# A two-layer Chebyshev graph network: one gathered chunk per step, an unrolled walk, a second table of h W2_1, dense stages that lag a visit each

## The chip, the cores and the metric

One NeuronCore of a Trainium2 chip. The metric is device time in microseconds, the median of plain runs, without the profiler.

## The reference

```
norm  = -dinv[src] * dinv[dst]                # dinv = 1/sqrt(number of edges leaving a node)
prop(h) = segment_sum(h[src] * norm, dst)     # 106250 edges sorted by dst, 6250 nodes
h1 = x @ W1_0 + prop(x) @ W1_1 + b1           # x: 6250 x 512 fp32, the weights 512 x 512
h  = leaky(layer_norm(h1) * gamma + beta)     # slope 0.01
y  = h @ W2_0 + prop(h) @ W2_1 + b2
out = layernorm(x + y)                        # without gamma and beta
```

Each node has 17 edges on average, so propagation is what costs: for every edge a row of 512 values is fetched by index and added into its node's row.

## The kernel before, in words

Nodes lie in 49 tiles of 128 (`TILES`), edges in 832 chunks of 128 (`CHUNKS`). The result must be near fp32, so a table in HBM holds every row as two fp16 halves, high and low, scaled by dinv and a power of two: `table[l]`, one per layer, 2 KB a row, 256 KB a chunk. One chunk is fetched by one indirect DMA on GpSimd (`L444`) into `ring`, 8 slots of a group of two chunks each.

**Steps.** Edges are sorted by destination, so a tile's edges are a run of groups. The walk has 464 steps per layer (`STEPS`): 416 groups (`GROUPS`) and 48 tile borders; a group on a border is stepped over once for each of its two tiles, but gathered once. Which tile and group a step has depends on the data: counts made in the start stage stand in `tile_i`, `group_i` and `slot_i` and are loaded into registers, 8 steps at a time. One step is: VectorE makes two one-hot matrices (edge x node in the tile, `L923`), PE multiplies them with the two chunks' high and low halves into one of 4 PSUM banks (`L710`, 4 matmuls), VectorE adds the bank, times `down` (dinv and the sign), to the tile's sums in `acc` (`L947`). `acc` holds all 49 tiles on chip.

PE may not write a bank before its add of four steps ago is done (`sums_added`). The sequence of a slot is relayed by SyncE: it waits for a group's landing, raises `groups_ready` for PE, waits for the step after which the slot is unused (`steps_done`, `L392`) and raises `ring_free` for GpSimd (`L393`). SyncE also copies the indices of 16 chunks at a time into `index` (`L371`).

**Blocks and visits.** The walk is run in blocks of 8 steps on PE and VectorE (`walk`, `L278`). After nearly every block each engine makes one *visit*, the dense stage of one tile whose sums must be complete by then; if an input's borders lay too late, `early` would send its visit behind the walk. The order of work in each engine's queue is that order of the code. On VectorE the one-hots of the next block stand right behind the visit (`prepare`). A visit in layer 0 is, for tile v:

```
...
                        for c in range(KB):
                            nc.tensor.matmul(to[:, :], base_in[:, tile_slot, c * P:(c + 1) * P],
                                             wB[:, c * D:(c + 1) * D], start=c == 0, stop=False)
                        pe.wait_ge(staged_ready, TILES * l + it.n + 1)
                        wait(pe, turned_moved, TILES * l + it.n)
                        turn(staged[tile_slot], bank[TURN_BANK], sums_turned)
...
                        pe.wait_ge(turned_moved, TILES * l + it.n + 1)
...
```

that is: PE multiplies the tile's features, read back already turned from `feat_dram`, with wB (`L727`); ScalarE copies the sums out of `acc` (`L546`); PE turns them with 4 transposes (`L655`, called from `L731`); ScalarE moves them to SBUF (`L564`); PE waits for that and multiplies with wA (`L749`); ScalarE copies the result to `acc` (`L613`). Other lines of the same visit work on older tiles: statistics (`L991`, `L994`), reciprocal and shift (`L958`, `L960`), normalising (`L556`), turning (`L736`), gamma and beta (`L598`), leaky (`L967`), turning back (`L742`), the split into high and low half (`L608`, `L974`), and the stores of features and of the second table. Layer 1's visit has the same two products and ends with the residual (`L983`), statistics and the output store. fp32 products take two PE instructions per 128 rows, so four blocks of weights are eight instructions. ScalarE issues the loads and stores of the visits.

Ahead of the walk a start stage of some 200 us loads x, counts degrees and borders, turns x into `feat_dram[0]` and writes the first table.

Of the kernel before, what the change touches and what calls it, by code (L numbers as in the profile page):

```python
# [17 lines left out]
WALK_FITS = "a step's tile is a count of at most TILES - 1 bounds, and its group the rest of its number"  # L39
# [36 lines left out]
def gnn_resnorm_kernel(nc, x, src, dst, w1_0, w1_1, b1, gamma, beta, w2_0, w2_1, b2, out):  # L76
# [7 lines left out]
    GROUP = 2  # L84
    GROUPS = -(-E // (GROUP * P))
    CHUNKS = GROUPS * GROUP
    STEPS = GROUPS + BOUNDS
    UNROLL = 8
    STEP_BLOCKS = STEPS // UNROLL
    GATHER_BLOCKS = GROUPS // UNROLL  # L90
    RING = UNROLL
    FREE_LAG = 4
# [3 lines left out]
    TABLE_VISIT = HIST_VISITS + 2  # L96
    LOAD = 7
    LOADS = TILES // LOAD
    FIRST_PLACE = 2
    PER = 6  # L100
    PERIODS = TILES // PER
    BIAS_PARTS = 3

    LAG_STATS, LAG_NORMAL, LAG_HIDDEN, LAG_LEAKY, LAG_BACK, LAG_LOW = 1, 2, 3, 4, 5, 6
# [4 lines left out]
    WALK = STEPS + 2 * UNROLL  # L109
    assert STEPS % UNROLL == 0 and GROUPS % (2 * UNROLL) == 0 and HIST * HIST_VISITS <= COLS  # L110
    assert HIST * HIST_VISITS * P >= E and TILES == LOADS * LOAD == 49 and CHUNKS <= COLS and TILES == PER * PERIODS + 1
    assert STEP_BLOCKS == FIRST_PLACE + (PER + 1) * PERIODS
# [6 lines left out]
    with ctx:  # L119
# [7 lines left out]
        ring = sb("ring", [P, RING * GROUP * ROW], FP16)  # L127
        wA = sb("wA", [P, KB * D], FP32)
        wB = sb("wB", [P, KB * D], FP32)
        work = sb("work", [P, 8 * D], FP32)  # L130
# [7 lines left out]
        count_i = sb("count_i", [P, WALK], I32)  # L138
        count = sb("count", [P, WALK], FP32)
        count_h = sb("count_h", [P, P], FP16)  # L140
        part_i = sb("part_i", [P, 1], I32)
        part = sb("part", [P, 1], FP32)
        thr = sb("thr", [P, TILES], FP32)
        onehot = sb("onehot", [P, UNROLL, GROUP, P], FP16)
        dst_c = sb("dst_c", [P, COLS], FP32)
        src_u = sb("src_u", [P, COLS], U32)
        src_lo = base_in[:, 0, 0:COLS // 2].bitcast(BF16)
        src_hi = base_in[:, 1, 0:COLS // 2].bitcast(BF16)
        index = sb("index", [P, 2, UNROLL * GROUP], U32)
        below = sb("below", [P, TILES], FP32)  # L150
        neg_tile = sb("neg_tile", [P, WALK], FP32)
        tile_i = sb("tile_i", [1, WALK], I32)
        group_i = sb("group_i", [1, WALK], I32)
        slot_i = sb("slot_i", [1, WALK], I32)
        used_i = sb("used_i", [1, GROUPS], I32)
# [864 lines left out]
```

## Time and profile before

| | |
|---|---|
| plain runs (3) | median 2442.14 us, 2441.22 to 2442.58 |
| profiled execution, span from first to last instruction | 3370.7 us |
| PE busy | 2065.1 us, 7250 matmuls |
| VectorE busy | 1544.4 us, 3507 instructions |
| ScalarE busy | 505.3 us |
| GpSimd busy | 1700.9 us, 1664 of them gathers |
| TensorE clock granted, mean | 0.780 |

No time of its own other than the span is recorded for the profiled execution. The span is far longer than the plain runs, so waits in the profile are not all waits of a plain run. "issue" is idle time that nothing in the records ends; "remote" is idle time ended by a semaphore of unknown origin. Matmul ends are modelled.

### The profile page before, as it was taken

How to read it: one execution, taken by the hardware profiler on the slowest of the kernel's cores; microseconds unless marked ns; L12 is line 12 of the kernel's file. 1: busy time of each engine (PE TensorE's matmuls, PEld its weight loads, DVE VectorE, ACT ScalarE, POOL GpSimd, SP SyncE). 2: the span in 40 equal slices, each digit the busy share in tenths (PEclk: the TensorE clock that was granted, in tenths of full speed). 3: DMA queues.
4: the chain of work that ended last, by engine and by line, in shares of the span. 5: the costliest groups of instructions: out<-in, count | busy, mean ns of one | idle time of the engine just before them, and what ended most of it. 6: DMA issues, size and time to landing. Idle time of an engine off the chain costs nothing.

```text
span 3370.7 us, 41016 instructions
## 1 busy us (share of the span) xinstructions
PE 2065.1 (61%) x7250; PEld 963.6 (29%) x7251; DVE 1544.4 (46%) x3507; ACT 505.3 (15%) x1030; POOL 1700.9 (50%) x1725
## 2 busy tenths in 40 slices
PE   6836576665665665665764656565565656555655
PEld 5712232222222322232331222222222222222222
DVE  6754444444444444544443444444444434444444
ACT  5920111111111211111230000000000000000000
POOL 0156554545555554655526545554545445554543
PEclk6558887887887878887876878787777777878778
DMA  6376565655555555655646555565555555555554
GB/s 215 133 259 181 150 174 155 173 159 160 164 167 168 159 165 157 181 159 167 182 132 200 166 158 171 166 177 155 167 159 164 155 158 165 161 165 162 159 159 122
DMA packets 215109, 559.98 MB, mean 166 GB/s; under 512 B 48100, under 2 KB 49760, under 8 KB 214948
## 3 DMA queue, kind: packets, MB, share of 16 engines
q0 software_dynamic: 133120, 436.31, 45.9%
q10 hardware_dynamic: 44676, 81.73, 7.2%
q1 hardware_dynamic: 37152, 40.21, 3.6%
q8 instruction: 50, 0.82, 0.1%
q14 instruction: 111, 0.91, 0.1%
HBM read 493.08 MB, written 64.18 MB: 165 GB/s over the span
## 4 chain that ended last, share of the span: by engine, by line
PE 30%; another core or an unknown queue 26%; issue 25%; DVE 8%; ACT 5%; DVEq 3%; ACTq 1%; DMA 1%; POOL 1%; SPq 0%; POOLq 0%
PE bank L749 16%; PE bank L710 10%; DVE acc L947 6%; PE bank L668 2%; ACT work L556 2%; ACT feat L564 1%; DVEq L923 1%; PE bank L727 1%; PE bank L655 1%; DVEq L947 1%; DVE onehot L923 1%; POOL ring L444 1%; ACT work L546 1%; ACTq L528 0%
## 5 line engine op out<-in xcount | busy, mean ns | idle before, releaser
L444 POOL DMA_INDIRECT ring<-table,index x1664 | 1672.6, 1005 | 1466.5 <-SPq L393 952.1
L947 DVE SCALAR_TENSOR_TENSOR acc<-bank,down,acc 128x512 f32 x928 | 696.9, 751 | 1219.6 <-PE bank L710 709.8
L710 PE MATMUL bank<-ring,onehot 128*128 x3712 | 920.3, 406 | 306.0 <-issue 148.1
L749 PE MATMUL bank<-wA,feat 128*128 128x512 f32 x784 | 547.6, 863 | 804.2 <-ACT feat L564 748.2
L923 DVE TENSOR_SCALAR onehot<-count_h,dst_c,neg_tile 128x128 f16<-128x128 f16 x1856 | 489.2, 329 | 490.1 <-issue 487.6
L710 PEld LDWEIGHTS bank<-ring,onehot 128*128 128x128 f16 x3712 | 380.6, 103 | 865.6 <-issue 515.3
L749 PEld LDWEIGHTS bank<-wA,feat 128*128 128x128 f32 x784 | 212.0, 285 | 1084.9 <-ACT feat L564 774.3
L727 PE MATMUL bank<-wB,base_in 128*128 128x512 f32 x784 | 353.6, 594 | 0.0
L546 ACT ACTIVATE work<-acc 128x512 f32 (+1 forms) x98 | 61.7, 630 | 1747.4 <-issue 1039.3
L727 PEld LDWEIGHTS bank<-wB,base_in 128*128 128x128 f32 x784 | 149.5, 191 | 155.8 <-issue 142.1
L564 ACT ACTIVATE feat<-bank 128x512 f32<-128x512 f32 x98 | 58.5, 597 | 845.4 <-remote 828.7
L655 PE MATMUL bank<-ident,work 128*128 128x128 f32 x588 | 88.3, 288 | 125.8 <-issue 99.7
L655 PEld LDWEIGHTS bank<-ident,work 128*128 128x128 f32 x588 | 67.1, 145 | 199.1 <-issue 181.7
L668 PE MATMUL bank<-ring 128*128 128x49 bf16 x864 | 85.2, 275 | 2.5 <-DVE ring L808 2.5
L668 PEld LDWEIGHTS bank<-ring 128*128 128x128 bf16 x864 | 83.6, 146 | 4.0 <-DVE ring L808 2.9
L598 ACT ACTIVATE feat<-bank,beta_c,gamma_c 128x128 f32<-128x128 f32 x196 | 73.8, 457 | 59.2 <-remote 39.5
L556 ACT ACTIVATE work<-acc,shift,rstd 128x512 f32 (+1 forms) x98 | 78.4, 800 | 6.6 <-DVE shift L960 3.0
L991 DVE BATCH_NORM_STATS2 stats<-acc 128x6 f32 (+1 forms) x98 | 67.5, 689 | 11.7 <-issue 9.5
L655 PE MATMUL bank<-ident,acc 128*128 128x128 f32 x196 | 52.4, 425 | 27.4 <-ACT feat L480 18.6
L805 DVE TENSOR_TENSOR ring<-work,base_in 128x4608 bf16<-128x4608 bf16 x24 | 61.4, 2559 | 14.4 <-PE bank L668 14.2
L421 POOL PARTITION_ALL_REDUCE row_max<-row_max x1 | 0.4, 382 | 126.0 <-DVE row_max L821 126.0
L613 ACT ACTIVATE acc<-bank 128x512 f32 (+1 forms) x49 | 29.4, 600 | 141.9 <-PE bank L749 132.7
(118 smaller groups left out, 689.6 us busy)
## 6 DMA issues: line engine op xcount, KB each, us to landing
ring<-table,index POOLq DMA_INDIRECT x1664
base_in<-feat ACTq DMA_DIRECT2D x98, 256.0 KB
feat<-feat SPq DMA_DIRECT2D x49, 256.0 KB, 2.9
table<-work SPq DMA_DIRECT2D x49, 256.0 KB, 3.1
feat<-feat ACTq DMA_DIRECT2D x49, 256.0 KB
table<-work ACTq DMA_DIRECT2D x49, 256.0 KB
feat<-in_x ACTq DMA_DIRECT2D x48, 256.0 KB
out<-work ACTq DMA_DIRECT2D x48, 256.0 KB
```

The lines of the kernel that those rows point to most:

```text
L444: nc.gpsimd.indirect_dma_start(out=ring[:, at * ROW:(at + 1) * ROW], out_offset=None, in_=table[l], in_offset=bass.IndirectOffsetOnAxis(ap ...
L546: nc.scalar.activation(staged[it.slot % 2], tile_of(acc, it.n), ACT.Copy).then_inc(staged_ready, 1)
L556: nc.scalar.activation(normed[s], tile_of(acc, k.n), ACT.Identity, bias=shift[:, k.slot % 3:k.slot % 3 + 1], scale=rstd[:, k.slot % 3:k.sl ...
L564: nc.scalar.activation(feat[:, 2 + s, :], bank[TURN_BANK][:, :], ACT.Copy).then_inc(turned_moved, 1)
L598: last = nc.scalar.activation(feat[:, s, c * P:(c + 1) * P], bank[NORMED_BANK][:, c * P:(c + 1) * P], ACT.Identity, bias=beta_c[:, c:c + 1 ...
L655: last = nc.tensor.transpose(to[:, c * P:(c + 1) * P], src_tile[:, c * P:(c + 1) * P], ident[:, :])
L668: last = nc.tensor.matmul(bank[4][:, 0:TILES], lo_hot[it.slot % 2][:, :, j], hi_hot[it.slot % 2][:, :, j], start=it.least == 0 and j == 0, ...
L710: last = nc.tensor.matmul(bank[u % SUM_BANKS][:, :], onehot[:, u, j, :], ring[:, bass.ds(at, D)], start=j + half == 0, stop=j + half == GROUP)
L727: nc.tensor.matmul(to[:, :], base_in[:, tile_slot, c * P:(c + 1) * P], wB[:, c * D:(c + 1) * D], start=c == 0, stop=False)
L749: last = nc.tensor.matmul(to[:, :], feat[:, 2 + tile_slot, c * P:(c + 1) * P], wA[:, c * D:(c + 1) * D], start=False, stop=c == KB - 1)
L923: last = nc.vector.tensor_scalar(onehot[:, slot, j, :], count_h[:, :], col(dst_c, group * GROUP + j), col(neg_tile, n), ALU.subtract, ALU. ...
L947: nc.vector.scalar_tensor_tensor(tile_of(acc, tile[u]), bank[u % SUM_BANKS][:, :], col(down[:, l, :], tile[u]), tile_of(acc, tile[u]), ALU ...
```

## The change

- One chunk per step (`GROUP = 1`): 832 + 48 = 880 steps per layer, and 880 gathers per layer, in the order of the steps. A chunk on a tile border is gathered twice. A table of indices for all 880 (`index`) and of destinations within the tile (`rel`) is made in the start stage by small fp32 matmuls with selection matrices (`pick`).
- The ring has 16 slots of one chunk. GpSimd and PE are unrolled, so slot addresses are constants, and both wait on the DMA's and PE's own semaphores. The relay and the index copies on SyncE are gone; SyncE issues the visits' loads and stores. The gather has no bounds check.
- One-hots: one VectorE instruction for 8 steps. The add into `acc` has no scale. Layer 0 scales while PE turns the sums (a product with a scaled identity in place of ScalarE's copy and 4 transposes); layer 1 scales in one VectorE instruction of its visit.
- The second table holds h W2_1 in place of h, since prop(h) W2_1 = prop(h W2_1). That product (wC) is in layer 0's visit; layer 1's visit has only the product with W2_0 and the bias, and no turn.
- In layer 0 turning the sums is the last piece of PE's visit of tile v; its products are made in visit v + 1, the turn of the normed tile in v + 2, wC's product in v + 3. Visits stand after the step `place(v)`, 18 steps apart; VectorE's and ScalarE's parts follow in their own order, VectorE's 9 steps later.

```
-    GROUP = 2
-    GROUPS = -(-E // (GROUP * P))
+    GROUP = 1
+    GROUPS = -(-E // (2 * P)) * 2 // GROUP
...
+    RING = 16
     SUM_BANKS = 4
...
+    SPACING = STEPS * 256 // TILES
+    FIRST_PLACE = -(-STEPS // TILES) + 8 // GROUP
+    STATS_LATER = -(-STEPS // TILES) // 2
+    LAG_SUMS, LAG_NORMAL, LAG_HIDDEN = 1, 2, 3
...
+            pool.wait_ge(index_ready, 1)
...
+                for c in range(GATHERS):
+                    n = GATHERS * l + c
+                    slot = n % RING
+
+                    wait(pool, steps_done, (n - RING) // GROUP + 1)
+                    nc.gpsimd.indirect_dma_start(
+                        out=ring[:, slot * ROW:(slot + 1) * ROW], out_offset=None, in_=table[l],
+                        in_offset=bass.IndirectOffsetOnAxis(ap=index[:, c:c + 1], axis=0)
+                    ).then_inc(ring_landed[slot], 16)
...
+            def pick_part(m):
+
+                n, half, b = m // (2 * EDGE_BLOCKS), m // EDGE_BLOCKS % 2, m % EDGE_BLOCKS
+                at = slice(half * HALF, (half + 1) * HALF)
+                return nc.tensor.matmul(pick_banks[n][half][:, 0:HALF_COLS].rearrange("p (n j) -> p n j", j=GROUP),
+                                        edge_f[n][:, b * P:(b + 1) * P], pick[b][:, at, :],
+                                        start=b == 0, stop=b == EDGE_BLOCKS - 1)
...
+            def step(l, n):
+                g = STEPS * l + n
+                for j in range(GROUP):
+                    c = g * GROUP + j
+                    slot = c % RING
+                    hot = onehot[:, n // BLOCK % 2, n % BLOCK * GROUP + j, :]
+                    if j == 0 and n % BLOCK == 0:
+                        pe.wait_ge(onehots_ready, g // BLOCK + 1)
+                    if g == 0 or n == 0:
+                        wait(pe, sums_added, g - SUM_BANKS + 1)
+                    pe.wait_ge(ring_landed[slot], 16 * (c // RING + 1))
+                    for half in range(2):
+                        if j == GROUP - 1 and half == 1 and n + 1 < STEPS:
+
+                            wait(pe, sums_added, g + 1 - SUM_BANKS + 1)
+                        last = nc.tensor.matmul(bank[n % SUM_BANKS][:, :], hot,
+                                                ring[:, slot * ROW + half * D:slot * ROW + (half + 1) * D],
+                                                start=j + half == 0, stop=j + half == GROUP)
+                last.then_inc(steps_done, 1)
...
+            def visit0(it, steps):
+                if it.within(LAG_NORMAL, TILES + LAG_NORMAL):
+
+                    k = it.back(LAG_NORMAL)
+                    pe.wait_ge(normed_ready, k.n + 1)
+                    pe.wait_ge(sums_moved, k.n + 2 if k.least + 1 < TILES else TILES)
+                    turn(normed[k.slot], bank[TURN_BANK], normed_turned)
...
+                    dense(bank[NEXT_BANK], feat[:, k.slot, :], wC, True).then_inc(next_done, 1)
...
+                    dense(to, base_in[:, k.slot, :], wB, False)
+                    bias(to, 0)
+                    pe.wait_ge(sums_moved, k.n + 1)
+                    for c in range(KB):
+                        last = nc.tensor.matmul(to[:, :], sums_t[k.slot][:, c * P:(c + 1) * P],
+                                                wA[:, c * D:(c + 1) * D], start=False, stop=c == KB - 1)
+                    last.then_inc(out_done, 1)
+                if it.within(0, TILES):
+
+                    pe.wait_ge(sums_added, steps)
+                    pe.wait_ge(diag_ready, it.n + 1)
...
+                        last = nc.tensor.matmul(bank[TURN_BANK][:, c * P:(c + 1) * P],
+                                                acc[:, bass.ds(it.n * D + c * P, P)], diag[:, it.slot, :],
+                                                start=True, stop=True)
+                    last.then_inc(sums_turned, 1)
...
+                    step(l, n)
+                    for v in range(TILES):
+                        if place(v) == n + 1:
+                            with pe.If(early > v):
+                                visit(numbered(v), n + 1)
...
+                nc.vector.tensor_tensor(onehot[:, b % 2, :, :], count_h[:, :].unsqueeze(1).to_broadcast([P, HOTS, P]),
+                                        rel[:, b * HOTS:(b + 1) * HOTS].unsqueeze(2).to_broadcast([P, HOTS, P]),
+                                        ALU.is_equal).then_inc(onehots_ready, 1)
...
+                for n in range(STEPS):
+                    g = STEPS * l + n
...
+                    at = dve.snap(tile[n % BLOCK] * D)
+                    dve.wait_ge(steps_done, g + 1)
+                    wait(dve, sums_added, g)
+                    nc.vector.tensor_tensor(acc[:, bass.ds(at, D)], acc[:, bass.ds(at, D)],
+                                            bank[n % SUM_BANKS][:, :], ALU.add).then_inc(sums_added, 1)
...
+                    for v in range(TILES):
+                        if place(v) + STATS_LATER == n + 1:
+                            with dve.If(early > v):
+                                visit(numbered(v), n + 1)
+                    if n % BLOCK == BLOCK - 1:
+                        hots(l, n // BLOCK + 2)
```

## Rows read from the trace of the kernel before

**Rows 1.** The page, chain that ended last, shares of the span by engine.

```profile
PE 30%; another core or an unknown queue 26%; issue 25%; DVE 8%; ACT 5%; DVEq 3%; ACTq 1%; DMA 1%; POOL 1%; SPq 0%; POOLq 0%
```

**Rows 2.** The page's groups: busy us, mean ns | idle before, releaser.

```profile
L444 POOL DMA_INDIRECT ring<-table,index x1664 | 1672.6, 1005 | 1466.5 <-SPq L393 952.1
L947 DVE SCALAR_TENSOR_TENSOR acc<-bank,down,acc 128x512 f32 x928 | 696.9, 751 | 1219.6 <-PE bank L710 709.8
L923 DVE TENSOR_SCALAR onehot<-count_h,dst_c,neg_tile 128x128 f16<-128x128 f16 x1856 | 489.2, 329 | 490.1 <-issue 487.6
```

**Rows 3.** Waits: engine and line, releaser, us in total, times, longest.

```profile
POOL ring L444 <- SPq L393: 952.1, 182, 11.6
ACT feat L564 <- remote: 828.7, 91, 13.3
```

**Rows 4.** Line 444 (gathers): min/median/max ns, first and last start.

```profile
L444 POOL DMA_INDIRECT ring<-table,index x1664: 996/1002/1901, 201.3 to 3333.2; - x185
```

**Rows 5.** Timeline between the layers: start us, length us, what, [idle before <-releaser].

```profile
1725.68 1.00 POOL L444 DMA_INDIRECT ring<-table,index  x1 [0.30 <-issue]
1728.34 0.60 ACT L564 ACTIVATE feat<-bank 128x512 f32<-128x512 f32 x1 [11.21 <-remote]
...
1744.95 0.60 ACT L564 ACTIVATE feat<-bank 128x512 f32<-128x512 f32 x1 [0.72 <-PE bank L655]
...
1774.87 1.00 POOL L444 DMA_INDIRECT ring<-table,index  x1 [48.19 <-issue]
```

**Rows 6.** Timeline, a block and a visit of layer 0.

```profile
902.68 5.29 PE L749 MATMUL bank<-wA,feat 128*128 128x512 f32 x8 [7.85 <-ACT feat L564]
...
907.81 7.07 PE L710 MATMUL bank<-ring,onehot 128*128 x32
...
913.60 1.00 POOL L444 DMA_INDIRECT ring<-table,index  x1 [0.31 <-issue]
913.96 0.75 DVE L947 SCALAR_TENSOR_TENSOR acc<-bank,down,acc 128x512 f32 x1 [0.24 <-DVE acc L947]
...
914.72 3.60 PE L727 MATMUL bank<-wB,base_in 128*128 128x512 f32 x8
...
920.91 0.60 PE L655 MATMUL bank<-ident,feat 128*128 128x128 f32 x4
...
921.45 0.39 PE L745 MATMUL bank<-bias_parts,ones_b 3*128 3x512 bf16 x1
921.50 0.18 DVE L994 BATCH_NORM_AGGREGATE mean_var<-stats 128x2 f32<-128x6 f32 x1 [0.15 <-issue]
922.42 1.95 DVE L923 TENSOR_SCALAR onehot<-count_h,dst_c,neg_tile 128x128 f16<-128x128 f16 x8 [0.73 <-issue]
```

**Rows 7.** Windows: PE, PEld, DVE, ACT, POOL busy, PEclk, DMA share, GB/s.

```profile
1724.00:1728.00 4.00, 0.00 (x0) 0.00 (x0) 0.00 (x0) 0.00 (x0) 2.08 (x3) 0.50 0.60 206
1733.00:1737.00 4.00, 4.00 (x18) 1.66 (x17) 1.50 (x2) 1.11 (x2) 0.00 (x0) 1.00 0.02 4
```

**Rows 8.** Groups by form, VectorE: busy us, mean ns | idle before.

```profile
L983 DVE TENSOR_TENSOR acc<-bank,feat 128x512 f32 x30 | 20.8, 692 | 3.5
L805 DVE TENSOR_TENSOR ring<-work,base_in 128x4608 bf16<-128x4608 bf16 x24 | 61.4, 2559 | 14.4 <-PE bank L668 14.2
L808 DVE TENSOR_TENSOR ring<-work,base_in 128x1764 bf16<-128x1764 bf16 x24 | 25.7, 1072 | 0.0
L991 DVE BATCH_NORM_STATS2 stats<-acc 128x6 f32 x60 | 41.3, 689 | 7.0 <-issue 6.8 <-DVE acc L983 0.2
L974 DVE SCALAR_TENSOR_TENSOR work<-bank,up,work 128x512 f16<-128x512 f32 x49 | 36.5, 745 | 4.0 <-ACT work L608 4.0
L967 DVE SCALAR_TENSOR_TENSOR feat<-feat 128x512 f32<-128x512 f32 x49 | 33.5, 684 | 8.7 <-ACT feat L598 8.7
L960 DVE TENSOR_SCALAR shift<-mean_var,rstd 128x1 f32<-128x1 f32 x98 | 21.0, 214 | 3.5
L958 DVE RECIPROCAL rstd<-std 128x1 f32<-128x1 f32 x98 | 15.0, 153 | 5.9 <-issue 3.0 <-ACT std L570 2.9
```

More of the change, by code:

```diff
@@ L38 @@
 EPS = 1e-5
-WALK_FITS = "a step's tile is a count of at most TILES - 1 bounds, and its group the rest of its number"
+WALK_FITS = "a step's tile is a count of at most TILES - 1 bounds"
 def wait(eng, sem, value):
@@ L404, in _ @@
+            for slot in range(2):
+                sp.wait_ge(s_out[slot], 16 * uses(slot, 2))
         @block.gpsimd
@@ new lines, in dense, with bias @@
+            def dense(to, x_of, w, stop):
+                for c in range(KB):
+                    last = nc.tensor.matmul(to[:, :], x_of[:, c * P:(c + 1) * P], w[:, c * D:(c + 1) * D],
+                                            start=c == 0, stop=stop and c == KB - 1)
+                return last
+            def bias(to, l):
+                return nc.tensor.matmul(to[:, :], ones_b[0:BIAS_PARTS, :], bias_parts[:, l * D:(l + 1) * D],
+                                        start=False, stop=l == 1)
@@ new lines, in visit1 @@
+            def visit1(it, steps):
+                if it.within(0, TILES):
+                    if it.least == 0:
+                        pe.wait_ge(s_wB[1], 16)
+                    to = bank[OUT_BANK + it.slot]
+                    wait(pe, kept, it.n - 1 if it.least > 1 else 0)
+                    pe.wait_ge(s_base_in[it.slot], 16 * (uses(it.slot, 2) + it.turn + 1))
+                    dense(to, base_in[:, it.slot, :], wB, False)
+                    bias(to, 1).then_inc(out_done, 1)
+            for l, visit, drain in ((0, visit0, LAG_HIDDEN), (1, visit1, 0)):
+                for n in range(STEPS):
+                    if l == 0 and n == NORM_STEP:
+                        pe.wait_ge(w_squared, 1)
+                        for b in range(KB):
+                            last = nc.tensor.matmul(bank[NEXT_BANK][:, :], ones_f[:, :], feat[:, b, :],
+                                                    start=b == 0, stop=b == KB - 1)
+                        last.then_inc(w_summed, 1)
+                    step(l, n)
[3 more added lines that the diff above has]
+                                visit(numbered(v), n + 1)
+                visits_late(pe, early, drain, visit, l == 0)
@@ L894, in _ @@
             link(nc.vector.tensor_copy(early_i[:, :], early_f[:, 1:2]))
-            dve.sem_inc(walk_ready, 1)
+            looped(dve, low_rows, 8, TILES - 1, 8)
+            straight(low_rows, TILES - 1, TILES, 8)
+            dve.wait_ge(picked, 1)
+            for half in range(2):
+                at = slice(half * HALF_COLS, (half + 1) * HALF_COLS)
+                last = nc.vector.tensor_scalar(index[:, at], pick_banks[0][half][:, 0:HALF_COLS], 0.0, None, ALU.max)
+            last.then_inc(index_ready, 1)
@@ L898, in _ @@
+            for b in range(2):
+                hots(0, b)
             dve.wait_ge(s_bias, 32)
@@ new lines, in visit1 @@
+            def visit1(it, _):
+                if it.within(1, TILES + 1):
+                    shifts(1, it.back(1))
+                if it.within(0, TILES):
+                    s = it.slot
+                    dve.wait_ge(out_done, TILES + it.n + 1)
+                    nc.vector.scalar_tensor_tensor(tile_of(acc, it.n), tile_of(acc, it.n), col(down[:, 1, :], it.n),
+                                                   bank[OUT_BANK + s][:, :], ALU.mult, ALU.add).then_inc(kept, 1)
+                    dve.wait_ge(s_resid[s], 16 * (it.turn + 1))
+                    dve.wait_ge(kept, it.n + 1)
+                    nc.vector.tensor_tensor(tile_of(acc, it.n), tile_of(acc, it.n), feat[:, 2 + s, :], ALU.add
+                                            ).then_inc(resid_added, 1)
+                    dve.wait_ge(resid_added, it.n + 1)
+                    wait(dve, shift_ready, TILES + it.n - 1 if it.least > 1 else 0)
+                    statistics(1, it.n, s, tile_of(acc, it.n))
```

687 lines of the change are left out of this document (301 added, 386 removed).

## The prediction

> **What bounds the kernel now.** I read the page first and then asked the trace four things: who waits for whom, where the gathers begin and end, what one stretch of layer 0 looks like in order of time, and what each form of instruction costs.
>
> The chain of waits names no single engine [rows 1], so it can't decide alone. The costliest group is the gather on GpSimd: 1664 indirect DMAs of 1005 ns mean [rows 2]. In the timeline a gather starts every 1.30 us when nothing holds it: 1.00 busy and 0.30 idle, which nobody releases [rows 6] (the row at 913.60). The first starts at 201.3, the last at 3333.2 [rows 4]; between the layers GpSimd idles 48.2 us [rows 5]. If nothing else held the gathers, the kernel would take 201.3 + 1664 x 1.305 (2171.5) + 48.2 + 37.5 (3370.7 less 3333.2) = 2458.5 us. The median of the plain runs is 2442.1, 0.7% less. The profiled execution's span is 3370.7; the only large thing that it has besides is 952.1 us in which GpSimd waits for a ring slot passed on by SyncE [rows 3], and 3370.7 less that is 2418.6. So the plain run lies where gathers run back to back, and the extra 930 us are waits that the profiled execution alone has. They are odd ones: ScalarE waits 828.7 us for a PE transpose whose matmuls stand in the records some 10 us earlier, always while gathers run; once they have stopped, the same wait is 0.7 us [rows 3, 5]. I take gather spacing and the durations of single instructions from the trace, and no waits of this kind; the sum is for the plain median, and on this kernel it is 0.7% high.
>
> How near are the others? A block of 8 steps holds 14.3 gathers on average (1664 / 116 blocks), 18.7 us. VectorE needs 8 adds at 0.75 + 0.24 (7.9 us) [rows 6] (the row at 913.96), 16 one-hots at 0.24 (1.95 us for 8 [rows 6], so 3.9), and its visit, 3.1 us, worked out below: 15 us. PE's visit (the dense stage of one tile) is about 9 to 11 us; VectorE does its one-hots and its own visit in just that time. So the gathers win, narrowly, and the two engines overlap by the order in which their work is placed.
>
> **The change part by part.**
>
> *Gathers.* 880 per layer instead of 832: a chunk on a tile's edge is gathered again for the next tile. 96 more x 1.305 = +125 us if gathers stay the limit. The relay through SyncE goes, and GpSimd waits on the steps themselves; that gains nothing where gathers run back to back. Whether the 0.30 gap shrinks, since the bounds register and the block loop go, no row shows: 0 to 0.30 us each. I keep 0.30, as the second gather of each pair, which has no wait ahead of it, shows it too.
>
> *VectorE's adds.* One add per step of one chunk instead of two: 1760 instead of 928. The scale moves out, so the form becomes TENSOR_TENSOR on a bank and SBUF, 692 ns [rows 8] (L983) against 751. The gap ahead of an add is 0.24 now [rows 6] (the row at 913.96). It holds two waits and the register work for three addresses; with one register address I bound it by 0.04 and 0.24 and take 0.19: 0.88 per add. A tile has 880 / 49 = 18.0 steps: 15.8 us per tile.
>
> *One-hots.* One TENSOR_TENSOR of 1024 fp16 elements for 8 steps instead of 16 small instructions. Two rows give this engine's slope where it packs 16-bit elements: (2559 - 1072) / (4608 - 1764) = 0.523 ns per element and 0.15 us fixed [rows 8]; the fp32 row gives (692 - 150) / 512 = 1.06. So 0.69 or 1.23 us. I take 1.23, because the index operand is one value repeated along the inner 128, which no row of the packed rate has. x 2.25 per tile = 2.8 us.
>
> The Trainium skill, "VectorE: DVE Perf Modes", section "What auto-detection actually checks", says that the packed mode wants every tensor 16-bit with a step of plus or minus 1; a repeated element has step 0. The two packed rows agree as far as they go (their repeated operand is repeated on an outer axis). By the rule the price is 1.23, without it 0.69, which would take 0.54 x 220 = 119 us off VectorE.
>
> The registers for 8 tiles are still loaded once per block: from the start of the 0.18 us op ahead to the first one-hot it is 0.92 us [rows 6] (the rows at 921.50 and 922.42). Behind a 1.23 us one-hot it is hidden; if not, +0.7 x 2.25.
>
> *VectorE's visit*, layer 0, once per tile: statistics 0.69 + 0.18, leaky 0.68, low half 0.745, reciprocal 0.15, shift 0.21 [rows 6, 8] = 2.66, with three gaps of 0.15: 3.1 us. Layer 1 the same within 0.1 (two adds in place of leaky and low half). Together VectorE has 15.8 + 2.8 + 3.1 = 21.7 us of work per tile, in both layers. The gathers of a tile take 18.0 x 1.305 = 23.4.
>
> *PE's visit.* Layer 0: products with wB, wA and now wC, 3.60 us each [rows 6] (the row at 914.72), bias 0.39, the turn of the normed tile 0.60, and the turn of the sums as a real product with a scaled identity, two passes where the transpose has one, 1.2: 13.0 us. It is one unbroken piece of PE's queue, because its inputs were made a visit earlier; that is what the lag buys: no waits inside. Two turns, the staging copy and the wait for it go. The steps' own matmuls fall from 3712 to 3520, 0.22 each, beside VectorE's work: nothing. Layer 1: wB and bias alone, 4.0 us; wA's product moved to layer 0 as wC, so the 3.60 are moved, not saved.
>
> *What the visit does to VectorE.* This is the term that decides. Adds come one per step from four banks, so PE can be at most three finished steps ahead when it enters a visit: 3 x 0.88 = 2.6 us of adds. A one-hot falls into that time in 3 of 8 visits (0.45). Then VectorE has nothing until PE has finished the visit and one step (0.43 + 0.22 to be seen). VectorE's own visit is placed 9 steps later, in the middle between two PE visits, and so overlaps none of it; before, it stood beside PE's. Idle per tile in layer 0: 13.0 - 2.6 - 0.45 + 0.65 = 10.6. A tile takes 21.7 + 10.6 = 32.3 us, and the gathers, at 23.4, fill the 16 slots and wait. 49 x 32.3 = 1583 us. Layer 1: 21.7 + 4.0 - 2.6 - 0.45 + 0.65 = 23.3, level with the gathers; 49 x 23.4 = 1149, and as two equal streams don't mesh I add 31: 1180.
>
> *Around them.* Start: the chunk table costs VectorE seven 880-element compares and PE 28 small products ahead of the first gather, some 15 us: 216. Between layers: one more tile through statistics, normalising, turn, activation, wC, split, store, about one drained visit shorter than now: 37 for 48. End: no turns, 15 for 37. DMA issues move from ScalarE to SyncE, whose queue is free of the relay; per tile that is three issues in 32 us, nothing.
>
> Sum: 216 + 1583 + 37 + 1180 + 15 = **3031 us**, 24% slower.
>
> Bounds. Low: gap 0.04, one-hot 0.69, visit 2.9 and PE's visit 12.2: 17.5 + (12.2 - 2.2 - 0.3 + 0.65) = 27.9 per tile, 1367, with layer 1 on the gathers at 1149: 2784. High: gap 0.24, loads not hidden (24.4 with a visit of 3.3), PE at the lower of its two clock levels when it enters a visit. The clock was granted at 0.50 after PE had been idle and at 1.00 while it was busy [rows 7]; the same eight instructions took 5.29 us after idling and 3.60 after steps [rows 6], so the visit is 14.7. 24.4 + 12.8 = 37.2 per tile and 26.5 in layer 1: 216 + 1823 + 37 + 1298 + 15 = 3389.
>
> **The rivals.**
> 1. *VectorE cheaper than I think*, the low sum: 2784. For it: one register address instead of three. Against: the gap has two waits in it either way.
> 2. *High sum*, PE's slow clock and register work in the open: 3389. For it: in the steps PE works only half the time (0.43 of 0.88). Against: before, the x32 group of steps ran at 7.07, 0.22 each, paced by VectorE too.
> 3. *Gathers stay the limit in both layers*: 216 + 2 x 1149 + 37 + 15 = 2566. It needs PE's visit to cost VectorE under 1.7 us per tile. For it: 16 slots of ring. Against: a ring lends time once; VectorE at 21.7 of 23.4 never pays back 10.6.
> 4. *Faster*: the 0.30 gap goes with the bounds register, 18.0 x 1.005 = 18.1 us per tile, and the visit is hidden, so that VectorE's 21.7 are all: 216 + 2 x 49 x 21.7 (2127) + 52 = 2395. The place is GpSimd's gap and PE's visit together. It decides from (2442 - 268) / 98 = 22.2 us per tile, averaged over both layers: the gather spacing has to fall below 1.23 and the visit's idle below 0.5. For it: nothing shows where the 0.30 comes from. Against: the four banks.
>
> **How the numbers follow.** Forecast 0.58 (its own range 2890 to 3180: 0.1 us either way on the add, 1 us on the visit), rival 1 0.16, rival 2 0.10, rival 3 0.08, rival 4 0.08. Rival 4 I split 0.06 faster and 0.02 within 0.2%, which is about what a measurement of this kernel can tell from no change; all else is slower: 0.92. The range 2700 to 3290 holds the forecast, rival 1 and half of rival 2, and leaves out rivals 3 and 4.
>
> **What would show it.** Right: in layer 0, VectorE idle some 10 us once in every 18 steps, ended by a PE step; gathers waiting for PE there and back to back in layer 1; the profile's layer 0 longer than its layer 1 by 300 us or more. Adds of 0.69 at 0.88 spacing; one-hots of 1.2 us x220; eight-instruction groups of 3.6 us on three lines in layer 0. Wrong: layers of equal length (rival 3 or 4), gather spacing near 1.0 (rival 4), one-hots of 0.69 (towards rival 1), PE's products at 5.3 us (rival 2). The forecast fails altogether if PE's visit is split, or if VectorE has other work to do during it.

## The result and the profile after

| | plain runs, median | range |
|---|---|---|
| kernel before, same chip (4 runs) | 2442.36 us | 2441.22 to 2443.38 |
| changed kernel (4 runs) | 2948.61 us | 2945.76 to 2950.69 |

The ratio is 1.2069, with a 95% interval of 1.2052 to 1.2086: 21% slower, 506 us. The forecast was 3031, 2.8% too high. The profiled execution has a span of 2943.9 us, 0.2% under the plain median, so this profile can be read as a plain run. That was not so before (3370.7 against 2442).

From the page of the changed kernel, the chain that ended last by engine, which answers to [rows 1], and the three groups that answer to those of [rows 2] (busy us, mean ns | idle before, releaser):

```profile
PE 42%; DVE 30%; issue 12%; DMA 8%; DVEq 3%; POOL 3%; ACT 1%; SPq 0%; ACTq 0%; POOLq 0%
...
L424 POOL DMA_INDIRECT ring<-table,index x1760 | 1776.8, 1010 | 944.7 <-PE bank L659 505.4
L1001 DVE TENSOR_TENSOR acc<-acc,bank 128x512 f32 x1760 | 1210.9, 688 | 970.5 <-PE bank L659 701.1
...
L904 DVE TENSOR_TENSOR onehot<-count_h,rel 128x1024 f16<-128x1024 f16 x220 | 268.2, 1220 | 0.2 <-DVE rel L892 0.2
```

PE and VectorE now carry the chain, and GpSimd's gathers wait for PE's steps. The window of each layer (PE, PEld, DVE, ACT, POOL busy, granted clock, DMA share, GB/s) shows that this is so in layer 0 only:

```profile
213.00:1704.00 1491.00, 1179.39 (x3495) 418.94 (x3495) 826.57 (x1274) 219.38 (x468) 881.38 (x880) 0.88 0.59 180
...
1780.00:2921.00 1141.00, 807.42 (x2151) 224.09 (x2151) 821.16 (x1245) 51.24 (x93) 878.22 (x863) 0.81 0.76 231
```

The same 880 gathers move 180 GB/s in layer 0 and 231 in layer 1. The timeline of one tile of layer 0, cut to a stretch around PE's visit (start us, length us, what, [idle before <-releaser]; PE's weight loads left out):

```profile
1156.91 0.69 DVE L1001 TENSOR_TENSOR acc<-acc,bank 128x512 f32 x1 [0.21 <-DVE acc L1001]
...
1157.51 1.22 DVE L904 TENSOR_TENSOR onehot<-count_h,rel 128x1024 f16<-128x1024 f16 x1
1158.47 1.07 POOL L424 DMA_INDIRECT ring<-table,index  x1 [0.30 <-PE bank L659]
1158.65 0.68 DVE L1001 TENSOR_TENSOR acc<-acc,bank 128x512 f32 x1
...
1159.61 0.63 PE L591 MATMUL bank<-ident,work 128*128 128x128 f32 x4
...
1160.08 3.60 PE L666 MATMUL bank<-wC,feat 128*128 128x512 f32 x8
...
1161.34 0.69 DVE L1001 TENSOR_TENSOR acc<-acc,bank 128x512 f32 x1 [0.21 <-DVE acc L1001]
...
1163.51 3.60 PE L666 MATMUL bank<-wB,base_in 128*128 128x512 f32 x8
...
1163.61 0.95 POOL L424 DMA_INDIRECT ring<-table,index  x1 [0.30 <-issue]
...
1167.36 3.70 PE L702 MATMUL bank<-wA,work 128*128 128x512 f32 x8
1170.89 1.05 PE L711 MATMUL bank<-diag,acc 128*128 128x128 f32 x8
...
1172.53 0.69 DVE L1001 TENSOR_TENSOR acc<-acc,bank 128x512 f32 x1 [10.50 <-PE bank L659]
1172.65 0.95 POOL L424 DMA_INDIRECT ring<-table,index  x1 [8.10 <-PE bank L659]
```

PE's visit runs without a gap from 1159.61 to 1171.78, 12.2 us. VectorE spends the finished steps that PE had ahead (last add at 1161.34) and then stands for 10.50 us. GpSimd fills the ring for two us more and stands for 8.10. In the waits between 300 and 1600 us (us in total, times, longest) this is the largest wait of either engine:

```profile
DVE acc L1001 <- PE bank L659: 447.6, 80, 12.5
...
POOL ring L424 <- PE bank L659: 380.9, 281, 9.8
```

42 of the 80 waits are visits, 438.9 us in all, and from the first to the last of them one comes every 30.81 us. That is 10.45 us of idle per tile and leaves 20.4 of work.

Between the layers, VectorE's and GpSimd's timelines (the answer to [rows 5]):

```profile
1679.40 1.23 POOL L424 DMA_INDIRECT ring<-table,index  x1 [0.30 <-PE bank L659]
1758.49 0.94 POOL L424 DMA_INDIRECT ring<-table,index  x1 [77.85 <-DMA table<-work]
```

```profile
1705.77 0.69 DVE L1001 TENSOR_TENSOR acc<-acc,bank 128x512 f32 x1 [0.21 <-DVE acc L1001]
1720.01 0.70 DVE L931 BATCH_NORM_STATS2 stats<-bank 128x6 f32<-128x512 f32 x1 [13.55 <-PE bank L702]
...
1736.88 0.70 DVE L931 BATCH_NORM_STATS2 stats<-bank 128x6 f32<-128x512 f32 x1 [14.28 <-PE bank L702]
```

And the gathers (shortest, median, longest in ns; first and last start), which answers to [rows 4]:

```profile
L424 POOL DMA_INDIRECT ring<-table,index x1760: 940/946/1997, 213.4 to 2920.7; - x196
```

In the forecast's own parts: start 213 (forecast 216), layer 0 from 213.4 to the last add's end at 1706.5, 1493 (1583), between the layers 52 (37), layer 1 from 1758.5 to 2920.7, 1162 (1180), end 23 (15).

### The profile page after: what moved, and what is told of

The parts are those of the page before. It is cut to its first block, busy times and chain, and to the rows that moved or that the text cites. A ratio compares the mean times of both kernels' runs of the same rounds, so it can differ in the third digit from the quotient of the medians.

```text
span 2943.9 us, 25416 instructions
## 1 busy us (share of the span) xinstructions
PE 2194.2 (75%) x6926; PEld 793.0 (27%) x6926; DVE 1840.8 (63%) x2761; ACT 426.3 (14%) x884; POOL 1805.4 (61%) x1821
## 4 chain that ended last, share of the span: by engine, by line
PE 42%; DVE 30%; issue 12%; DMA 8%; DVEq 3%; POOL 3%; ACT 1%; SPq 0%; ACTq 0%; POOLq 0%
DVE acc L1001 24%; PE bank L666 18%; PE bank L659 10%; DMA ring<-table,index 7%; PE bank L702 6%; POOL ring L424 3%; PE bank L612 3%; DVEq L1001 2%; PE bank L591 2%; DVE stats L931 2%; PE bank L711 1%; DVE work L965 1%; PE bank L671 1%; DMA table<-work 1%; DVEq L24 1%
## 5 line engine op out<-in xcount | busy, mean ns | idle before, releaser
L424 POOL DMA_INDIRECT ring<-table,index x1760 | 1776.8, 1010 | 944.7 <-PE bank L659 505.4
L1001 DVE TENSOR_TENSOR acc<-acc,bank 128x512 f32 x1760 | 1210.9, 688 | 970.5 <-PE bank L659 701.1
L659 PE MATMUL bank<-ring,onehot 128*128 128x512 f16 x3520 | 1216.1, 460 | 677.5 <-DVE acc L1001 555.0
L659 PEld LDWEIGHTS bank<-ring,onehot 128*128 128x128 f16 x3520 | 259.2, 101 | 1598.1 <-DVE acc L1001 1277.3
L904 DVE TENSOR_TENSOR onehot<-count_h,rel 128x1024 f16<-128x1024 f16 x220 | 268.2, 1220 | 0.2 <-DVE rel L892 0.2
L666 PE MATMUL bank<-wC,feat 128*128 128x512 f32 x392 | 188.4, 626 | 1.7 <-DVE work L965 1.7
L702 PE MATMUL bank<-wA,work 128*128 128x512 f32 x392 | 181.3, 605 | 0.0
L666 PEld LDWEIGHTS bank<-wC,feat 128*128 128x128 f32 x392 | 78.0, 211 | 79.5 <-issue 79.5
L702 PEld LDWEIGHTS bank<-wA,work 128*128 128x128 f32 x392 | 70.4, 189 | 81.4 <-issue 81.4
L711 PE MATMUL bank<-diag,acc 128*128 128x128 f32 x392 | 52.7, 278 | 3.1 <-DVE acc L1001 3.1
```

The lines of the kernel that those rows point to most:

```text
L424: nc.gpsimd.indirect_dma_start(out=ring[:, slot * ROW:(slot + 1) * ROW], out_offset=None, in_=table[l], in_offset=bass.IndirectOffsetOnAxi ...
L659: last = nc.tensor.matmul(bank[n % SUM_BANKS][:, :], hot, ring[:, slot * ROW + half * D:slot * ROW + (half + 1) * D], start=j + half == 0, ...
L666: last = nc.tensor.matmul(to[:, :], x_of[:, c * P:(c + 1) * P], w[:, c * D:(c + 1) * D], start=c == 0, stop=stop and c == KB - 1)
L702: last = nc.tensor.matmul(to[:, :], sums_t[k.slot][:, c * P:(c + 1) * P], wA[:, c * D:(c + 1) * D], start=False, stop=c == KB - 1)
L711: last = nc.tensor.matmul(bank[TURN_BANK][:, c * P:(c + 1) * P], acc[:, bass.ds(it.n * D + c * P, P)], diag[:, it.slot, :], start=True, st ...
L904: nc.vector.tensor_tensor(onehot[:, b % 2, :, :], count_h[:, :].unsqueeze(1).to_broadcast([P, HOTS, P]), rel[:, b * HOTS:(b + 1) * HOTS].u ...
```

## The experiments

Theory: in layer 0 one unbroken visit of PE empties VectorE's lead of steps; what it lasts beyond the lead is lost, 49 times. Rivals: the gathers limit both layers, or VectorE's own work does. The runs came on three occasions, each on another chip, and the first was unlike the others: there the kernel before takes 3368.83 us in plain runs (7 runs, 3361 to 3390), where it takes 2444.36 and 2441.10 on the other two. Whether the chip or the moment makes that difference was not separated; it is called the chip's below. Each ratio is against the kernel before on the same chip.

**The visit's order, and the visit split (first occasion).** Both cut PE's visit into eight pieces in a new order; one puts all pieces in one place, as the change does, the other spreads them two steps apart and moves VectorE's part behind them. Nothing is left out: the products are the same in number and kind.

```
+    LATER = (9, STATS_LATER)
...
+            ORDER = ((base_low, base_high, sums_low, sums_high, turn_normed, next_low, next_high, turn_sums))
+            PIECE_AT = (0, 0, 0, 0, 0, 0, 0, 0)
...
+                            due = [p for p, at in zip(ORDER, PIECE_AT) if min(place(v) + at, STEPS) == n + 1]
```

That is order_only. split_visit differs from it in two lines:

```
+    LATER = (16, STATS_LATER)
...
+            PIECE_AT = (0, 2, 4, 6, 8, 10, 12, 14)
```

`LATER` is the number of steps by which VectorE's part follows the visit's place, in layer 0 and in layer 1.

> Control for the next run: the changed kernel with the pieces of PE's layer-0 visit in another order (wB, bias, wA, turn of the normed tile, wC, turn of the sums), still in one piece at the same step. All theories: within 15 us of 2949. If the order itself matters, the next run must be read against this one.

> The same order as the control, but the visit cut into eight pieces of at most 1.7 to 1.9 us that stand two steps apart (0, 2, ... 14 steps after the visit's place), VectorE's visit at 16. The same instructions, nothing left out. Theory: each piece is shorter than the 2.6 us of stored adds, so VectorE's idle falls from 10.6 us to 0 to 2 per tile and layer 0 comes down to the gathers, 880 x 1.31 = 1153 us for 1493; 2610 to 2660 in all. Rival 1 (gathers bound layer 0 already): no change. Rival 2 (VectorE's own work): no change.

**A quarter of wC's product, and half an add (first occasion).** The first leaves three of four blocks of wC's product out, the second adds only 256 of 512 columns.

```
-                    dense(bank[NEXT_BANK], feat[:, k.slot, :], wC, True).then_inc(next_done, 1)
+                    nc.tensor.matmul(bank[NEXT_BANK][:, :], feat[:, k.slot, 0:P], wC[:, 0:D], start=True, stop=True
+                                     ).then_inc(next_done, 1)
```

```
+                    nc.vector.tensor_tensor(acc[:, bass.ds(at, D // 2)], acc[:, bass.ds(at, D // 2)],
+                                            bank[n % SUM_BANKS][:, 0:D // 2], ALU.add).then_inc(sums_added, 1)
```

> The changed kernel with one of the four blocks of the product with wC left out of none but three: only block 0 is computed (the rest of the product is left out, so PE's visit in layer 0 is 6 PE instructions shorter, 0.427 us each by the wB groups, 2.6 us). Theory (PE's unbroken visit starves VectorE, which has at most three adds stored up): VectorE's idle stretch per tile goes from 12.5 to about 10, 49 x 2.6 = 127 us less in all, 2822 us. Rival 1 (the gathers and their 16 slots bound layer 0): no change, 2949. Rival 2 (VectorE's own instructions bound both layers, the visit only seems to): no change.

> The changed kernel whose add into the sums takes 256 of the 512 columns (the other half of the sums is left out); an add is then about 0.42 us in place of 0.69. Theory: layer 0 loses 18 x 0.27 less 3 x 0.27 (the stored adds are shorter too) = 4.1 us per tile, 199 us; layer 1 is bound by the gathers and loses 0 to 30 us; 2720 to 2750 in all. Rival 1 (gathers bound both layers): no change, 2949. Rival 2 (VectorE's own work bounds both layers): 1760 x 0.27 = 475 us less, 2474.

| first occasion | median us | ratio to before (3368.83) |
|---|---|---|
| order_only | 3062.88 | 0.908 [0.904, 0.912] |
| split_visit | 2849.33 | 0.845 [0.841, 0.849] |
| quarter_wC | 2945.01 | 0.874 [0.870, 0.878] |
| half_add | 2899.56 | 0.861 [0.856, 0.865] |

The times expected were sized for a chip on which the kernel before takes 2442, and missed. The order of the three cuts is the expected one (the split gives most, then half an add, then the quarter), but what this occasion shows first is another thing: here the change, with no more than its visit reordered, is 9% faster than the kernel before. The waits of order_only between 1900 and 2900 us say what is odd:

```profile
DVE acc L1046 <- PE bank L660: 95.4, 51, 5.3
DVE acc L1046 <- remote: 91.9, 31, 5.5
```

About half of the time that VectorE waits for PE here has lost its releaser, as [rows 3] had for ScalarE in the kernel before. So the profile of before most likely came from a chip of this kind: its 3370.7 is what the kernel takes there in plain runs too (3368.83). The sizes of the mechanism had to be measured again elsewhere.

**The change again, the bounds check, and the node row in PSUM (second occasion; before 2444.36).** The first run is the changed kernel unaltered. after_check gives the gather its bounds check back. psum_node lets layer 1's one-hots read the row of node numbers from a PSUM bank, copied there once between the layers, so that only one operand is in SBUF.

```
+                        in_offset=bass.IndirectOffsetOnAxis(ap=index[:, c:c + 1], axis=0),
+                        bounds_check=bound, oob_is_err=False).then_inc(ring_landed[slot], 16)
```

```
+                node = bank[NEXT_BANK][:, 0:P] if l == 1 else count_h[:, :]
+                nc.vector.tensor_tensor(onehot[:, b % 2, :, :], node.unsqueeze(1).to_broadcast([P, HOTS, P]),
```

> The changed kernel itself, unaltered, because the kernel before took 3369 us in the last four comparisons and 2442 us in the one that gave the result. If that is a property of the chip or of the occasion, the changed kernel has two times as well: where before is 3369, the theory of the visit asks for 2945 (one block of three left out) + 127 = about 3070; where before is 2442, 2949 again. If instead the kernel before alone has two times, this one stays at 2949 beside a before of 3369, and the three runs with nothing or little changed (2945, 3063) contradict the theory.

> The changed kernel with the gather's bounds check put back, as before had it. One gather then takes 1.00 us in place of 0.945. Layer 1 is bound by the gathers: 880 x 0.056 = 49 us more; layer 0 is not, 0 more. Rival (gathers bound both layers): 98 us more. Rival (the check costs nothing, the 0.945 comes from constant addresses): no change.

> The changed kernel with the row of node numbers that the one-hot compares against read from a PSUM bank (fp32) in layer 1 instead of from SBUF (fp16), so that VectorE's one-hot has only one operand in SBUF there. Gathers that run beside a one-hot took up to 1.8 us in place of 0.945, 0.065 on the mean of all. If two SBUF operands hold the gather's start, the mean in layer 1 goes from 1.02 to about 0.95 and layer 1 loses some 50 us; if the stretch comes from something else (any long VectorE instruction, DMA traffic), no change.

The change again: 2947.79, ratio 1.205 [1.203, 1.208]. With the check: 2968.24, 20 us more where 49 were expected. With the node row in PSUM: 2911.60, 36 less where 50 were expected. The gathers of layer 1 between 1900 and 2250 us, of after_again, of after_check and of psum_node (busy us, mean ns | idle before):

```profile
L424 POOL DMA_INDIRECT ring<-table,index x264 | 271.3, 1028 | 80.4 <-issue 53.3 <-PE bank L659 27.1
```

```profile
L425 POOL DMA_INDIRECT ring<-table,index x259 | 271.5, 1048 | 79.0 <-issue 52.7 <-PE bank L660 26.2
```

```profile
L424 POOL DMA_INDIRECT ring<-table,index x279 | 265.7, 952 | 85.3 <-issue 58.2 <-PE bank L659 27.1
```

All three run back to back, busy or in the 0.30 gap for the whole 350 us. psum_node's mean falls to 952 ns, the shortest 940: the 76 ns between 1028 and 952 were the one-hots' doing. Its timeline shows a gather beside a one-hot, no longer than any other, and one beside the add of the residual, which still has both its inputs in SBUF:

```profile
2000.27 0.69 DVE L982 TENSOR_TENSOR acc<-acc,feat 128x512 f32<-128x512 f32 x1
2000.48 1.30 POOL L424 DMA_INDIRECT ring<-table,index  x1 [0.30 <-issue]
...
2007.08 0.94 POOL L424 DMA_INDIRECT ring<-table,index  x1 [0.30 <-issue]
2007.30 1.22 DVE L905 TENSOR_TENSOR onehot<-bank,rel 128x1024 f16<-128x1024 f32 x1
2008.33 0.94 POOL L424 DMA_INDIRECT ring<-table,index  x1 [0.30 <-PE bank L659]
```

In the changed kernel the gather at 1158.47 took 1.07 us and ended 0.81 after the one-hot's end at 1158.73; others took up to 2.0. In layer 1 of psum_node 186 gathers run beside a one-hot and none takes over 0.95 us, while 26 beside L982 take 1.05 to 1.45 and all end 0.81 to 0.83 after it. The edit changed the node row's type too (fp16 to fp32), but L982 is fp32 throughout and stretches gathers, so the wider type by itself does not spare them. The one-hot is 1.22 us in both. From first to last gather, layer 1 of psum_node is 1116.6 us against 1166.4 of the change on the same chip, 50 less, as expected; but 11 come back behind the last gather (33.6 against 23.0) and 4 ahead of the first. VectorE, close behind the gathers, is late there: it has 16 adds to make after the last gather's start, where after_again has 9. after_check's layer 1 is 19 us longer (1185.8) and its mean 20 ns, though its shortest gather rises 52 ns (940 to 992), which is 46 us for 880. The rest is in the stretched ones: 120 of layer 1's gathers exceed the shortest by more than 50 ns in after_again, by 68 us together, and 100 in after_check, by 42. Why they are fewer stays open. In layer 0 neither change in the gather can be felt (first gather to last add 1494 us in after_again, 1490 and 1497 in the two others): the gathers wait there anyway.

The Trainium skill, "SBUF — State Buffer", section "Who interferes with whom", says that a VectorE instruction with two inputs in SBUF contends with a GpSimd instruction that reads SBUF. The two traces agree: 952 ns with one input in SBUF, 1028 with two.

**The kernel before without its bounds check (second occasion).**

```
-                                in_offset=bass.IndirectOffsetOnAxis(ap=index[:, it.slot, at:at + 1], axis=0),
-                                bounds_check=bound, oob_is_err=False).then_inc(ring_landed[k], 16)
+                                in_offset=bass.IndirectOffsetOnAxis(ap=index[:, it.slot, at:at + 1], axis=0)
+                                ).then_inc(ring_landed[k], 16)
```

> The kernel before with the gather's bounds check left out (and two of its register loads, PE's group numbers and SyncE's, asserted to be in range, which adds some short sequencer instructions). If plain runs of before were bound by gathers back to back, each 0.056 us shorter, where before takes 2442 this takes 1664 x 0.056 = 93 us less, 2350. Where before takes 3369 it waits for slots, and a shorter gather gains 0 to 30 us.

Measured 2359.93, ratio 0.965 [0.964, 0.967]: 84 us less where 93 were expected. Its gathers and its chain:

```profile
L442 POOL DMA_INDIRECT ring<-table,index x1664: 942/946/1920, 201.4 to 2332.8; - x185
```

```profile
issue 33%; DMA 25%; POOL 23%; PE 12%; SPq 3%; DVE 1%; ACT 1%; POOLq 1%; ACTq 0%; DVEq 0%
```

A kernel of 1664 gathers that gains 84 us from 52 ns each (mean 1005 in [rows 2] to 953, 87 us) is bound by its gathers. This is also the fastest version of the study: it beats both kernels.

**The sizes, where the kernel before is gather-bound (third occasion; before 2441.10).** The changed kernel and three of the kernels of the first occasion again.

> The changed kernel, unaltered, as the base of this comparison: 2948 us where before takes 2442; where before takes 3369, about 3070 by the theory of the visit (the order control took 3063 there, and the run with a shorter visit 2945).

> The visit in eight pieces again, to be read against the changed kernel on the same chip. Where before takes 2442: idle of VectorE per tile from 10.6 to 0 to 2 us, layer 0 down to the gathers at 880 x 1.31; 2610 to 2660. Where before takes 3369: 2849 as measured.

> One block of wC's product for four (the other three left out), against the changed kernel on the same chip: 49 x 2.6 = 127 us less by the theory of the visit, no change by both rivals. Where before takes 2442 that is 2821, else 2945.

> The add on 256 of 512 columns (half the sums left out), against the changed kernel on the same chip: layer 0 199 us less, layer 1 0 to 30 less by the theory; 475 less if VectorE's own work bound both layers; nothing if gathers did. Where before takes 2442: 2720 to 2750.

| third occasion | median us | against the change | expected | ratio to before |
|---|---|---|---|---|
| after_third | 2946.91 | | | 1.207 [1.205, 1.210] |
| split_visit_2 | 2605.64 | -341 | 2610 to 2660 | 1.068 [1.066, 1.070] |
| quarter_wC_2 | 2816.56 | -130 | 2821 | 1.154 [1.152, 1.156] |
| half_add_2 | 2771.96 | -175 | 2720 to 2750 | 1.135 [1.133, 1.137] |

*A quarter of wC.* Six of eight instructions at 0.43 are 2.6 us of visit, and the 49 tiles lost 130 us. In the traces 116.5 of it lie in layer 0 (1492.2 us from the first gather to the last add in after_third, 1375.7 here), where 45 of the 49 products with wC stand, and 11.1 between the layers (51.9 to 40.8), where the other 4 are made: 2.6 and 2.8 for each. PE's visit stands in layer 0's time at full price. If the gathers, or VectorE's work, limited that layer, this run would have shown nothing. Of VectorE's waits for PE between 300 and 1500 us 43 are visits, 338.7 us, 7.88 each for 10.45:

```profile
DVE acc L1002 <- PE bank L659: 348.8, 84, 9.8
```

*Half an add.* An add takes 421 ns for 688, 4.8 us per tile of 18. Three of them lie in PE's visit, so 4.0 should be gained 49 times, 196. Measured 175, outside the range expected. The idle per visit grew from 10.45 to 11.5 (504.8 us in 44 visits between 300 and 1500), 1.0 where 0.8 was forecast, and the shorter waits for PE from 0.2 to 0.6 us per tile; a visit comes every 27.19 us for 30.81, 3.6 less. Layer 1 did not move: 261 gathers between 1900 and 2250 for 264, and PE waits there for landings (busy us, mean ns | idle before):

```profile
L424 POOL DMA_INDIRECT ring<-table,index x261 | 271.3, 1039 | 79.5 <-issue 58.2 <-PE bank L659 21.3
L659 PE MATMUL bank<-ring,onehot 128*128 128x512 f16 x520 | 189.4, 485 | 104.7 <-DMA ring<-table,index 100.8 <-DVE acc L1001 2.6
```

So in layer 0 VectorE's work and PE's visit are in series, and in layer 1 the gathers are the limit.

*The split.* It takes no instruction away and wins 341 us, 337 of them in layer 0 (1492.2 to 1155.2). It also has another order and VectorE's part 7 steps later than the change; the control for the order ran on the first chip only (next table). The window of layer 0 and the waits of VectorE, PE and GpSimd in it (300 to 1600 us):

```profile
300.00:1300.00 1000.00, 885.53 (x3096) 398.53 (x3095) 723.72 (x1112) 197.16 (x424) 766.91 (x766) 0.98 0.78 234
```

```profile
DVE acc L1046 <- PE bank L660: 237.9, 281, 7.7
...
PEld bank L660 <- DMA ring<-table,index: 184.2, 188, 4.9
...
POOL ring L425 <- PE bank L660: 83.5, 274, 0.3
```

GpSimd's longest wait for PE is 0.3, its ordinary gap; in the changed kernel it was 9.8. PE waits for landings. Layer 0 moves 234 GB/s, as layer 1 of the change does (231), and its last gather ends at 1361 us: (1361 - 213) / 880 = 1.305 us per gather.

What is left between the split kernel (2606) and the one before (2441) is 165 us. Of the kernel before there is no trace at 2441, so the stages around its gathers are taken from before_no_check: 96 more gathers at 1.305 (125), 14 more between the layers (51.75 idle for 37.9), 11 at the start (212.8 for 201.4), and layer 1's spacing of 1.322 for 1.305 (880 x 0.017 = 15), which is the stretch beside two-input instructions; 2 less at the end (24.9 for 27.0). That makes 163; it is a sum of estimates, not a measurement.

**The same kernels on the two kinds of chip, by layer.** Layer 0 from the first gather to the end of the last add, layer 1 from its first to its last gather, us, from the traces:

| | layer 0, first occasion | layer 0, third | layer 1, first occasion | layer 1, third |
|---|---|---|---|---|
| the change | | 1492.2 | | 1164.5 |
| order_only | 1519.1 | | 1258.7 | |
| quarter_wC | 1394.5 | 1375.7 | 1257.4 | 1160.9 |
| half_add | 1340.8 | 1324.6 | 1261.2 | 1162.9 |
| split_visit | 1295.1 | 1155.2 | 1260.8 | 1162.0 |

The first chip's extra time lies where gathers are the limit: 96 to 99 us in each layer 1 and 140 in the split kernel's layer 0, but only 16 and 19 in a layer 0 that PE's visit holds. There the theory's sizes nearly fit on the first chip too: against order_only a quarter of wC takes 125 us off layer 0 and half an add 178; against the change on the third they take 116 and 168. And the control settles the order: order_only's layer 0 is 27 us above the change's on the third, of which 16 to 19 are the chip's, so the new order by itself costs layer 0 some 10 us and gives 13 back between the layers (38.7 in order_only, 52.0 in half_add on the same chip). On balance it wins nothing of the 341. This is an estimate, as the change itself did not run on the first chip; that VectorE's part stands 7 steps later has no control of its own.

## Why the prediction was right or wrong

**What bounded the kernel before.** Right that plain runs are gather-bound: before_no_check showed it. Wrong in one claim, "the extra 930 us are waits that the profiled execution alone has". On one of the three chips of the experiments plain runs of before take 3368.83, so the waits don't need the profiler. The choice to leave them out of the sum fitted the chip that was measured, and that was luck: on the other chip the forecast's sign would have been wrong, since there order_only is 9% faster than before. That case was in no rival. The sum for the kernel before was 0.7% high because two of its terms came from the slow kind's trace: before_no_check has 37.9 us between the layers for 48.2, and 27.0 after the last gather for 37.5, which makes 2438.

**Gathers.** 1760 and a gap of 0.30, right. Not foreseen: the check's 0.05 us went from the duration (1005 to 953 ns in the kernel before), and VectorE instructions with two SBUF inputs, one-hots above all, gave some 0.07 back on average. The two cancel, by luck, so that layer 1's spacing, (2920.7 - 1758.5) / 879 = 1.322, came out near the 1.305 taken. The 31 us that I added because "two equal streams don't mesh" stood for the wrong thing; psum_node showed it to be the stretch, 50 us.

**VectorE's work.** Forecast 21.7 per tile, measured 20.4. Adds 0.688 as taken from [rows 8], spacing 0.90 where 0.88 was said: 16.2 for 15.8. The one-hot is 1.220, forecast 1.23; the rule of the Trainium skill that was weighed ("VectorE: DVE Perf Modes", "What auto-detection actually checks") holds here, and rival 1's 0.69 falls. But it costs the queue only 0.84: from the add at 1156.91 to the next at 1158.65 are 1.74, less 0.90. An instruction that waits for nothing begins before the one ahead has ended in the records (1157.51 against 1157.60), and the next add needs no gap. So 1.9 for 2.8. VectorE's visit likewise costs about 2.3 for 3.1; I had charged three gaps of 0.15. This step was mis-sized, by 1.3 of the 1.5 us by which a tile was too long (30.81 for 32.3), some 64 of the 90 us in layer 0. Most of the rest is the count: the forecast charges 49 whole visits, but PE's 49th stands behind the last step (`place` gives 880), and the first ones lack pieces whose inputs come a visit or two later (waits of 6.2 and 8.5 us at 281 and 309).

**PE's visit and what it does to VectorE.** Visit 12.2 for 13.0: turns of 0.5 and 0.9 us, products of 3.4 to 3.5. Idle 10.45 forecast as 10.6; the lead of three adds, the missing one-hots and the position of VectorE's part were as described. The clock was granted at 1.00 in such a visit:

```profile
1160.00:1171.00 11.00, 11.00 (x29) 4.75 (x27) 1.61 (x3) 2.48 (x6) 3.64 (x4) 1.00 0.45 141
```

Rival 2's products at 5.3 hardly showed: of 123 such groups of eight in layer 0 one took over 5 us (5.07). That the visit decides layer 0 was tested from three sides and stood.

**Start, between, end.** 213 for 216. Between the layers 52 for 37, which was taken down from 48.2, GpSimd's idle time there, while the 52 run from VectorE's last add; GpSimd's idle time is 77.9. Two visits run drained, one after the other, each with 13.6 to 14.3 us in which VectorE waits for PE's product; I had counted "one more tile" as one shorter visit. End 23 for 15.

**Sum.** Layer 0 -90, layer 1 -18, start -3, between +15, end +8: -88 on 3031 is 2943, the span.

**Rivals.** 3 (gathers limit both layers, 2566) fell for the change, and is what the split makes of it, at 2606. 4 needed a gather spacing under 1.23; it is 1.25 at best.

## What to carry to other kernels

An engine that feeds others through a few slots must not take a long piece of other work in one go: the piece costs its length less the lead in the slots, every time, and cutting it into pieces no longer than that lead, a few steps apart, takes the cost away with the same instructions (341 us here). Before dividing or repeating work, ask which stream is the limit: this change gave the limit, the gathers, 96 more, and gave VectorE more to do as well (busy 1841 us for 1500 in before_no_check), since each chunk now has an add of its own. And if the profiled span and the plain time differ by a third, run both kernels on another chip before choosing one.

## What the runs showed of the hardware

- Two plain times for one kernel on three chips: 2441 and 2444 us on two, 3369 on the third. The changed kernel differs far less (2947 against 3063 for its reordered form). The extra time stands where gathers are dense: some 97 us in each layer 1 of 880 gathers. In the traces of the slow kind part of PE's releases of other engines are recorded as unknown, and in that of the kernel before ScalarE's waits for PE end some 10 us late while gathers run (11.21 and, once they have stopped, 0.72 [rows 5]). The cause is open and was not tried.
- The bounds check of an indirect DMA costs 0.05 us of GpSimd's time each (shortest 992 against 940 ns in the changed kernel, mean 1005 against 953 in the one before).
- An indirect DMA on GpSimd that is held beside a VectorE `TENSOR_TENSOR` with two SBUF inputs lasts until 0.80 to 0.83 us after that instruction's end (188 gathers beside one-hots in the changed kernel, 26 beside the residual's add in psum_node's layer 1), up to 2.0 us in all. Beside one-hots with one input in SBUF none of 186 is longer than 0.95. The kernel before made its one-hots one by one with a single tensor input; without the check its gathers have a mean of 953.
- Back-to-back VectorE instructions with no wait between them overlap by 0.08 to 0.09 us in the records.
